# Two extra transposes ahead of the attention output matmuls, and the first activation load of the last feed-forward stage split in two

## The reference

```python
q, k, v = x @ Wq, x @ Wk, x @ Wv                  # x: (8, 2048 tokens, 2048 features)
scores = einsum('bes,bfs->bef', q.T, k.T) / 8     # features x features
attn   = softmax(scores, -1) @ v.T                # then transposed back
x = layernorm(x + attn.T @ Wo)
w1_q, w2_q = sign(w) * (|w| >= 0.7*mean|w|)       # both quantized to -1, 0, 1
h = gelu(x @ w1_q.T + b1)                         # 2048 x 8192
x = layernorm(x + h @ w2_q.T + b2)
```

## Time and profile before

| | us |
|---|---|
| median of the timed runs | 4139.82 (two: 4130.69 and 4148.95) |
| the profiled execution's own time | 3589.69 |
| its span, slowest core (7) | 3588.2 |
| spans of the 8 cores | 3559.2 to 3588.2 |
| PE busy in the span | 3203.2 |
| stage p3, matmuls and transposes | from 1091.0 to about 1378 |
| stage f2, first DMA issued, first matmul | 2582.9, 2611.6 |

### The profile page before, as it was taken

The page is one execution under the profiler, slowest core; times in us unless marked ns, Lnnn a source line. Parts: engine busy times, 40 slices in busy tenths (PEclk is TensorE's granted clock), DMA queues, the critical chain, the costliest instruction groups (busy, mean ns, idle before and its releaser), DMA issues.

```text
span 3588.2 us, 37270 instructions; the slowest of 8 cores (3559.2 to 3588.2 us)
## 1 busy us (share of the span) xinstructions
PE 3203.2 (89%) x14917; PEld 1447.7 (40%) x14917; DVE 1240.8 (35%) x1362; ACT 731.3 (20%) x1065; POOL 99.3 (3%) x174
## 2 busy tenths in 40 slices
PE   0998899995995996996999999999779999899997
PEld 0443344442442442443444444444334444344442
DVE  0111221112555951554334343433213333333333
ACT  1344454230111221453111111111100000200003
POOL 0000000000000000000000000000000000000000
PEclk9999999997997998997999999999889999899997
DMA  9899997565547745665565656565543323732312
GB/s 198 213 282 284 274 289 242 164 205 121 149 147 260 264 144 125 227 234 177 180 189 184 198 179 201 189 190 183 189 172 141 126 86 141 258 116 95 141 71 94
DMA packets 357757, 656.83 MB, mean 183 GB/s; under 512 B 177296, under 2 KB 234704, under 8 KB 333008
## 3 DMA queue, kind: packets, MB, share of 16 engines
q1 hardware_dynamic: 238880, 299.95, 26.2%
q0 software_dynamic: 41776, 184.60, 18.8%
q10 hardware_dynamic: 76928, 169.89, 14.2%
HBM read 536.98 MB, written 150.99 MB: 192 GB/s over the span
## 4 chain that ended last, share of the span: by engine, by line
PE 49%; DMA 3%; ACT 0%; DVE 0%; issue 0%; ACTq 0%; DVEq 0%; SPq 0%
PE psH L982 25%; PE psF L1090 24%; DMA w2g<-w2q_h 1%; DMA y<-outt 1%; PE psF L1082 0%; DMA w1sl<-w1q_h 0%; DVE outt L1115 0%; ACT lnsink L1174 0%; DMA h_h<-hstg 0%; DVE oacc L1140 0%; ACT hstg L999 0%; ACT mr_t L1196 0%; ACT rstd_t L1194 0%; ACT st L1183 0%; ACT st L1180 0%
## 5 line engine op out<-in xcount | busy, mean ns | idle before, releaser
L1090 PE MATMUL psF<-w2g,hg 128*128 128x512 bf16 x4096 | 907.1, 385 | 9.6 <-DMA w2g<-w2q_h 9.6
L982 PE MATMUL psH<-big,w1sl 128*128 128x512 bf16 x4096 | 887.0, 380 | 12.3 <-DMA w1sl<-w1q_h 12.3
L1090 PEld LDWEIGHTS psF<-w2g,hg 128*128 128x128 bf16 x4096 | 404.1, 99 | 512.3 <-issue 71.8
L982 PEld LDWEIGHTS psH<-big,w1sl 128*128 128x128 bf16 x4096 | 401.4, 98 | 497.5 <-issue 16.0
L1140 DVE TENSOR_TENSOR oacc<-psF,oacc 128x2048 f32<-128x2048 f32 x112 | 256.5, 2291 | 593.4 <-PE psF L1090 593.4
L456 ACT ACTIVATE sbin<-sbin 128x1024 f32<-128x1024 f32 x256 | 269.0, 1051 | 411.4 <-DMA sbin<-w1t 191.6
L325 PE MATMUL psA<-wbuf,big 128*128 128x512 bf16 x1024 | 231.9, 388 | 103.6 <-DMA wbuf<-wq 96.4
L229 DVE TENSOR_TENSOR qout<-qmask,qout 128x1024 bf16<-128x1024 f32 x256 | 311.6, 1218 | 0.0
L999 ACT ACTIVATE hstg<-psH,b1sb 128x2048 bf16<-128x2048 f32 x64 | 125.9, 1967 | 745.1 <-PE psH L982 745.1
L702 PE MATMUL psO<-big,atsl 128*128 128x512 bf16 x1024 | 225.4, 381 | 45.4 <-DMA big<-v_h 24.8
L325 PE MATMUL psB<-wbuf,big 128*128 128x512 bf16 x1024 | 228.4, 385 | 24.6 <-DVE spillb L371 24.6
(11 more groups left out here) (115 smaller groups left out, 1338.9 us busy)
## 6 DMA issues: line engine op xcount, KB each, us to landing
w2g<-w2q_h SPq DMA_DIRECT2D x15, 4096.0 KB, 14.3
sbin<-w2t SPq DMA_DIRECT2D x76, 512.0 KB, 6.8
sbin<-w1t SPq DMA_DIRECT2D x64, 512.0 KB, 8.3
sbin<-w1t ACTq DMA_DIRECT2D x64, 512.0 KB, 8.8
qin<-w1t POOLq DMA_DIRECT2D x32, 1024.0 KB, 7.0
w1q_h<-qout SPq DMA_DIRECT2D x64, 512.0 KB, 3.4
w1sl<-w1q_h SPq DMA_DIRECT2D x64, 512.0 KB, 5.6
qin<-w2t POOLq DMA_DIRECT2D x32, 1024.0 KB, 7.7
```

What stands on the lines that cost most here:

```text
L982: mm = t.matmul(ps[:, nb * 512:nb * 512 + 512], w1sl[:, (f_m % 2) * 2048 + d_k * P: (f_m % 2) * 2048 + d_k * P + P], big0[:, d_k * S + nb ...
L1090: mm = t.matmul(ps[:, nb * 512:nb * 512 + 512], hg[:, slot * 8192 + f_k * 1024 + j * P: slot * 8192 + f_k * 1024 + j * P + P], w2g[:, slot ...
```

## The change

It has two parts.

In p3, `trsp(2)` and `trsp(3)` are moved ahead of the first matmuls; behind the matmuls of tiles 0 and 1 there are then no transposes, and from tile 2 on all is as it was. Nothing is added: the moved transposes wait for the same ACT copies (`a_trs` 1 and 2) as before.

In f2, the first load of `hg` is cut in two: ACT issues strips 0 to 3 (1 MB) and behind it `w2g` strips 4 to 7 as before; SP issues `hg` strips 4 to 7 (1 MB) as `s_misc` item 2, behind its half of `w2g` and ahead of the eight `oacc` loads. PE waits for the new item where it waits for item 1, ahead of strip 4 of the first tile.

```diff
@@ block p3, tensor @@
                                 trsp(0)
                                 trsp(1)
+                                trsp(2)
+                                trsp(3)
                                 for e_m in range(nE):
...
-                                    if e_m + 2 < nE:
+                                    if e_m >= 2 and e_m + 2 < nE:
                                         trsp(e_m + 2)
@@ block f2, sync, grp_loads, gi == 0 @@
                             s_w2g.issue_idx(
                                 sy, w2g[:, 0:8192],
                                 hap(w2q_h, 0, [[E, P], [P * E, 4], [1, E]]), 0)
+                            s_misc.issue_idx(
+                                sy, hg[:, 4096:8192],
+                                hap(h_h, 4 * P * S,
+                                    [[S, P], [P * S, 4], [1, 1024]]), 2)
@@ block f2, tensor @@
                                     if gi == 0 and j == 0 and f_k == 4:
                                         s_misc.wait_item(t, 1)
+                                        s_misc.wait_item(t, 2)
@@ block f2, scalar @@
                     s_hg.issue_idx(
-                        s, hg[:, 0:8192],
-                        hap(h_h, 0, [[S, P], [P * S, 8], [1, 1024]]), 0)
+                        s, hg[:, 0:4096],
+                        hap(h_h, 0, [[S, P], [P * S, 4], [1, 1024]]), 0)
```

## The result

| | us |
|---|---|
| the changed kernel, median of 16 runs | 3561.56 |
| the kernel before, median of 15 runs, the two shown ahead among them | 3584.3 |
| ratio of the two, 95% interval | 0.9939 (0.9919 to 0.9959) |
| the changed kernel's profiled execution, its span | 3565.15, 3563.6 |

The change makes the kernel 22 us faster, 0.6%; the interval leaves 15 to 29 us. The two runs shown ahead of the prediction, 4130.69 and 4148.95, are of a kind that comes up among the changed kernel's runs too (4148.76, with the cores of one die at a granted clock of 0.81), while ten of the thirteen runs of the kernel before that were taken later lie at 3573 to 3603; the ratio leaves such runs out.

The account below looks back on a forecast made before the run. PE's chain of matmuls bounds the kernel, so only PE's waits can be won: 0 in p3 plus 25.0 us in f2, taken from 4139.82, makes 4114.8 us, range 4095 to 4140.

Parts of the forecast that it names:

- the same 25.0: Whole kernel: the f2 gain of 25.0 us, taken from the timed median 4139.82 as from the profiled 3589.69.
- The fourth rival: Whole kernel: timed executions differ in kind from the profiled one, tens to hundreds of us either side; chance 0.05.
- two sets moved away win 2 x 0: p3, gaps between tiles: ACT's 1.97 us is late with or without transposes, so moving two sets gains 0 us.
- the pause costs nothing: p3, emptied gaps: PE's longer idle time of 2.21 us does not cost its clock, 0 us.
- the sign named for it: p3: 64 matmuls taking over 14 us behind an unfilled gap would show the forecast wrong.
- my bound of 3.7: p3: slow starts behind two unfilled gaps lose 2 x 1.83 = 3.7 us at most.
- The second rival: p3: the pauses do cost PE its clock, 3.7 us back, 4118.5 us; chance 0.05.
- The start at 13.1 us: Start of f2: both first loads are in 13.1 us after issue, at 2596.0, and PE starts there instead of 2611.64.
- the far end: f2, first tile: second 3.15 MB take 13.1 us, second 16 matmuls begin at 2609.1 at slow clock; gain 19.9 us.
- What is late next: f2 behind the first tile: `oacc` and group 1 loads land in time, so nothing gives the 25 us back.
- The third rival: f2, group 0: `oacc`'s first tile lands only at 2646.0, PE's third tile waits 31.4 us, 4146.2 us; chance 0.05.
- nor the first: f2, first rival: `oacc` moves beside the new `hg` piece, `w2g` lands at 2614.8, gain 14.2, 4125.6 us; chance 0.10.

Follow-up runs that it names:

- p3_only: The kernel before with only the p3 transposes moved and f2 as before; ratio to the kernel before 1.0007.
- tail_on_act: The kernel before with only the f2 change, but `hg` strips 4 to 7 issued by ACT behind its half of `w2g`; ratio 0.9997.
- preload_real: The kernel before with group 0's `w2g` loaded in f1, 16 unread transposes in p3's last gap, 24 unread full-row matmuls starting f2; ratio 0.9876.

## Why the prediction was right or wrong

**The level: wrong.** "I take the same 25.0 from 4139.82" is the step that failed. The gain in proportion was right, 4114.8 of 4139.82 being 0.9940 where 0.9939 was measured, but the time given, 4115, lies 553 us above the measured median. I had seen that the two runs stood 550 us above the profiled execution, and wrote that no row told why. That very excess should have told me which of the two to trust: the profile's own clock of 0.958 to 0.964 and its 3589.69 us were an execution that I could read line by line, the other two were not. The fourth rival named this case, at 0.05 in all and outside the stated range. It deserved most of the chance, or a range that reached down to 3565. The kernel before came out at 3584.3, and from there the same 25.0 us would have made 3559.3, 2.3 below what was measured.

**p3: the cover was right, the clock was not.** That "two sets moved away win 2 x 0" held to the hundredth (2.11 us). The wait for V covered the moved sets as forecast (28.1 us from the first transpose to the first matmul, 28.3 before). That the pause costs nothing failed, and the sign named for it came up: on core 7 the 64 matmuls behind the second unfilled gap took 15.66 us. I had taken the 0 from one gap on one core. In the 16 gaps of the changed kernel it costs 7 x 1.69 = 11.8 us over 8 cores, 1.5 us a core, within my bound of 3.7. The second rival, at 0.05, is in part what happened. `p3_only`'s ratio, 1.0007, agrees in its sign, but can't show a cost of 0.04%.

**f2: the mechanism right, two terms too good.** The start at 13.1 us was 13.5 on core 7 and 12.3 in the mean. The second loads were to land together 22.5 us after the first issue; on core 7 SP's came after 21.6 and ACT's after 24.4, 2.1 us late for the start of the second 16 at 24.6. And these were to take 3.5 us, since the pause before was short; they took 6.47 behind a pause of 3.28 us, 2.9 us more; even the far end had put in only the 4.97 us of the profile before for the slow clock. 25.0 - 2.1 - 2.9 = 20.0, what core 7 shows. In the mean over the cores it is 23.2, less 1.5 in p3: 21.7 us, and the measured ratio makes 0.0061 x 3584 = 21.9. With an interval of 15 to 29 us, that the two agree so closely is luck.

**What is late next: right.** No wait of PE for DVE in group 0, none at group 1. The third rival did not occur, nor the first: `oacc` stayed behind the new piece, as `tail_on_act` shows from the other side, where it is `oacc` that takes the engines.

## What to carry to other kernels

When PE waits for a load and the DMA engines are already full, don't ask on which queue the load is but what runs beside it and with how long rows: each of two busy queues got a share that goes with its row length, for rows of 2 to 8 KB, so that a prefetch in 8 KB rows took 3.22 of 4.12 MB from a load in 2 KB rows. Hold the prefetch back, which here took two waits and gained at least as much as the split, or move part of the needed bytes into an earlier stage. And before filling or emptying a gap of TensorE count what it does to its clock on every core, since one core and one gap can show either.

## What the runs showed of the hardware

- An unfilled pause of PE of 2.2 us between two series of matmuls cost 1.6 to 1.7 us of slow clock in 41 of 104 cases (15 of 32 and 26 of 72), and a pause of the same length with 16 transposes in it in none of 1336.
- Two busy DMA queues moved the same number of packets, 444 and 443 in 12 us, with 0.90 and 3.22 MB in them: rows of 2 KB got 22% of the bytes beside rows of 8 KB.
- The clock stayed down under matmuls with one row of weights: 34 of them at 431 ns each, in 14.66 us, and slow real ones behind them. Under 24 with 128 rows of weights, on core 1 of `preload_real`, it rose: they took 8.24 us, and what followed ran at full clock. On core 3 the clock was still up when they began, behind the same 3.16 us of rest, and they took 5.34 us, 222 ns each.
- The clock can rise on transposes alone. In the changed kernel on core 7 PE idles for 11.74 us, runs the first two sets of 16 transposes slow and the next two, 1.7 us later, at full clock; here the second set and the third. The third ran at full clock on 5 of the 8 cores, slow on the others.

```profile
1102.62 1.91 PE L683 MATMUL psTB<-ident_bf,big 128*128 128x128 bf16 x16
1106.22 1.05 PE L683 MATMUL psTA<-ident_bf,big 128*128 128x128 bf16 x16 [1.68 <-ACT atsl L728]
```

The Trainium skill (TensorE: Matmul & The Clock Gate, Part 4) says that the full clock does not engage for transposes; these rows show otherwise, and the measurement decides.
